# First edge gather of a graph network: sums kept with nodes on the lanes instead of features on the lanes

## Chip, cores and metric

The kernel is one program on one core of one Trainium2 chip, written instruction by instruction for each engine with explicit semaphores. The metric is device time in microseconds (us) of the whole program, the median of several executions.

## What is computed

The reference is a two-layer graph network on 6,250 nodes of 256 features: a message-passing layer over 100,000 edges, a mixture of 8 experts, a five-layer message-passing network over the same edges, and a second mixture whose gate is a graph attention over 65,536 edges. The part that the change touches is the first message passing:

```python
# x: (6250, 256); src, dst: (100000,); edge_weight: (100000,)
xn = _layernorm(x)
messages = xn[dst] * edge_weight[:, None]
agg = segment_sum(messages, src, num_segments=N)
h = xn + agg
out = relu(h @ W1 + b1) @ W2 + b2
x = x + out
```

Everything is in f32. What the change must deliver to the next stage is `h`, turned: `sh.agg` of shape [128, 2, 6272], with the feature within its block of 128 on the lanes (partitions), then the block of features, then the node.

## The kernel before

The program is a row of phases with a barrier of all engines between them; `first_sums` is the third, called p3 in the names of the profile. By then the edges are sorted by their target node into windows of 128 nodes (NT = 49 windows) and cut into NC1 = 832 chunks of 128 edges, each chunk within one window. `listA` holds for every edge the row to fetch, its place in its window and its weight.

`first_sums` walks the 832 chunks in 52 turns. A turn has S = 4 sets of U = 4 chunks. Each set has its own buffer `rows[s]` for fetched node rows, `hot[s]` for the matrices and `idx[s]` for the indices. The engines share the work like this:

- ACT (`Gather.act_set`) waits until TensorE has used up set s of the turn before (semaphore `used`, one count per chunk), then copies the four index columns to `idx[s]` (line 302).
- POOL (`Gather.pool_set`, line 308) waits for that copy, then issues four indirect DMAs, each of which fetches 128 rows of 1 KB of the table `xn0` to `rows[s][:, u, :]`.
- DVE (`Aggregate._matrices`, line 369) builds a 128x128 matrix for each chunk, which has the edge's weight at (edge, place in window), one set ahead; and (`_sums`, line 379) adds each finished product to the window of `sh.agg` that a register names. The registers are loaded four at a time (`windows_of`). Each add waits for the product and for the add before it.
- TensorE (`pe_set`, line 393) waits for the matrices (`hot_ready`), for the rows (`here`) and for each PSUM bank to be free (`added[u]`), and multiplies: for each of the two blocks of features the block of rows is the stationary operand and the matrix the moving one with 128 columns. The result has the features on the lanes and the nodes along them.
- The term `xn` itself comes in through `AddTurned`. In each of the first 49 turns SP loads one tile of 128 rows of `xn0` (two buffers), TensorE turns its two blocks (line 1802) after its own turn's products, and DVE adds them to `sh.agg` (line 1810) after its own turn's adds. TensorE's loop holds two turns for this, so that the two buffers alternate.

An f32 product or load of weights is recorded as two instructions, so a chunk shows four MATMUL and four LDWEIGHTS rows.

After the phase's barrier comes `first_ffn` (p4), whose `Ffn` reads `sh.agg`, while POOL issues scatters for a later stage (line 263).

## Time and profile before

| | |
|---|---|
| median of 3 runs | 14222.39 us (14183.71 to 14226.25) |
| the profiled execution: time, span | 14220.56 us, 14218.8 us |
| TensorE's granted clock, mean over the span | 0.766 |
| busy share of the span: PE, DVE, POOL, ACT | 53%, 46%, 52%, 9% |
| phase p3, from the memset's start to the last add's end | 1509.76 to 2800.40 us |
| in it: chunks, matmul rows, adds of line 379 | 832, 3328, 832 |

PE is TensorE's matmul row, PEld its loads of weights, DVE the vector engine, ACT the scalar engine, POOL the engine that issues the indirect DMAs, and SP the one that issues the plain ones. PEclk is the clock that TensorE was granted, as a share of 2.4 GHz. An idle time marked "issue" is one in which the engine waited for nothing that the profile shows; one marked "remote" has a releaser that the profile can't name.

### The profile page before, as it was taken

Reading aid. Unit: us, or ns where it says so; the run is one execution under the profiler, and the core shown is the slowest. Engines: PE = TensorE matmul, PEld = TensorE weight load, DVE = VectorE, ACT = ScalarE, POOL = GpSimd, SP = SyncE. Lnnn points to the kernel's source line nnn. Section 1 sums busy time; section 2 is a strip of 40 time slices with the busy share of each in tenths; the row PEclk is TensorE's granted clock in tenths of the full one; section 3 lists DMA queues with packets and bytes.
Section 4 is the critical chain, followed back from the end, with each engine's and each line's share of the span. In section 5 each row is a group of like instructions: output and inputs, shape, how many; then the busy total and the mean of one; then the engine's idle time right before and its main releaser. Section 6 shows DMA issues by size and latency. Waiting matters only on the chain. (4 is left out here: it accounts for less than half of the span.)

```text
span 14218.8 us, 158198 instructions
## 1 busy us (share of the span) xinstructions
PE 7586.1 (53%) x34918; PEld 5503.2 (39%) x34919; DVE 6529.1 (46%) x18936; ACT 1314.3 (9%) x3588; POOL 7369.4 (52%) x7692
## 2 busy tenths in 40 slices
PE   0002355552139677765655465555554655378877
PEld 0002344431026444444544344444443444233355
DVE  7336544411015356654444344434443444345566
ACT  0000000001001100001000100010001000123342
POOL 5772466635740255564666566656665666445400
PEclk9999866675569788877776777677776766578988
DMA  1000233211000133322333233323332333211203
GB/s 58 20 1 1 71 91 91 82 43 48 2 7 21 57 81 83 82 73 63 88 87 87 67 87 87 87 69 86 88 87 67 85 88 87 58 21 21 23 11 102
DMA packets 518785, 873.35 MB, mean 61 GB/s; under 512 B 180375, under 2 KB 355656, under 8 KB 517579
## 3 DMA queue, kind: packets, MB, share of 16 engines
q0 software_dynamic: 323968, 674.90, 18.6%
q1 hardware_dynamic: 194635, 196.60, 4.4%
q14 instruction: 138, 1.13, 0.0%
q8 instruction: 44, 0.72, 0.0%
HBM read 771.76 MB, written 105.62 MB: 62 GB/s over the span
## 5 line engine op out<-in xcount | busy, mean ns | idle before, releaser
L308 POOL DMA_INDIRECT p_layers_place<-nodesC,p_layers_idx x4160 | 3942.5, 948 | 2937.6 <-issue 1573.7
L393 PE MATMUL p_layers_bank<-p_layers_hots,p_layers_place 128*128 128x128 f32 x16640 | 3366.7, 362 | 2863.4 <-DVE agg L379 1513.9
L393 PEld LDWEIGHTS p_layers_bank<-p_layers_hots,p_layers_place 128*128 128x128 f32 x16640 | 2869.0, 257 | 3452.7 <-issue 1933.9
L379 DVE TENSOR_TENSOR agg<-agg,p_layers_bank 128x256 f32 x4160 | 1751.5, 421 | 2282.3 <-issue 858.9
L369 DVE TENSOR_SCALAR p_layers_hots<-iota,p_msg_edges 128x128 f32<-128x128 f32 x3328 | 997.6, 363 | 759.9 <-issue 599.8
L308 POOL DMA_INDIRECT p_gather_rows<-xn,p_gather_idx x832 | 788.3, 947 | 822.7 <-ACT p_gather_idx L302 578.6
L263 POOL DMA_INDIRECT listC<-h x782 | 777.1, 994 | 526.1 <-issue 253.0
L393 PE MATMUL p_agg_bank<-p_agg_hot,p_gather_rows 128*128 128x128 f32 x3328 | 685.9, 374 | 594.2 <-DVE agg L379 372.9
L263 POOL DMA_INDIRECT listA<-h x782 | 812.7, 1039 | 344.4 <-issue 341.0
L263 POOL DMA_INDIRECT listD<-recD,rowD x512 | 493.1, 963 | 785.3 <-issue 785.3
L393 PEld LDWEIGHTS p_agg_bank<-p_agg_hot,p_gather_rows 128*128 128x128 f32 x3328 | 602.8, 271 | 677.9 <-issue 373.6
L488 PE MATMUL p_ffn_y<-p_ffn_w,p_ffn_hid 128*128 128x256 f32 x1960 | 489.7, 409 | 649.9 <-issue 623.7
L302 ACT COPY p_layers_idx<-p_msg_edges 128x4 int32 x1040 | 203.0, 197 | 6378.9 <-PE p_layers_bank L393 2779.4
L1369 POOL DMA_INDIRECT gat_att_rows<-nodesD,gat_att_idx x560 | 529.2, 945 | 477.7 <-ACT gat_att_idx L1399 291.2
L488 PEld LDWEIGHTS p_ffn_y<-p_ffn_w,p_ffn_hid 128*128 128x128 f32 x1960 | 395.6, 205 | 753.1 <-issue 670.0
L530 DVE SCALAR_TENSOR_TENSOR p_ffn_acc<-p_ffn_y,p_mix_share,p_ffn_acc 128x256 f32<-128x256 f32 x392 | 189.4, 483 | 901.2 <-remote 591.4
L1642 DVE TENSOR_REDUCE gat_att_red<-gat_att_bank 128x4 f32<-128x512 f32 x560 | 373.8, 687 | 412.3 <-PE gat_att_bank L1481 200.6
L379 DVE TENSOR_TENSOR agg<-agg,p_agg_bank 128x256 f32 x832 | 350.3, 421 | 416.6 <-issue 165.8
L475 PE MATMUL p_ffn_pre<-agg,p_ffn_w 128*128 x1120 | 457.1, 562 | 137.7 <-ACT p_ffn_hid L509 68.3
L365 DVE SCALAR_TENSOR_TENSOR p_layers_hots<-iota,p_msg_edges,p_msg_dinv_row 128x128 f32<-128x128 f32 x832 | 273.5, 352 | 219.9 <-issue 132.0
L396 PE MATMUL p_layers_bank<-p_layers_hots,p_layers_attr 128*4 128x128 f32 x1664 | 364.7, 307 | 0.0
L475 PEld LDWEIGHTS p_ffn_pre<-agg,p_ffn_w 128*128 128x128 f32 x1120 | 222.7, 199 | 346.8 <-issue 271.5
(387 smaller groups left out, 8125.2 us busy)
## 6 DMA issues: line engine op xcount, KB each, us to landing
p_layers_place<-nodesC,p_layers_idx POOLq DMA_INDIRECT x4160
nodesC<-p_layers_place SPq DMA_DIRECT2D x24, 896.0 KB, 4.7
part_y<-rows SPq DMA_DIRECT2D x21, 896.0 KB
agg<-part_y SPq DMA_DIRECT2D x18, 896.0 KB, 10.3
p_gather_rows<-xn,p_gather_idx POOLq DMA_INDIRECT x832
x<-p_ffn_acc SPq DMA_DIRECT2D x14, 896.0 KB, 4.1
listA<-h POOLq DMA_INDIRECT x782
listC<-h POOLq DMA_INDIRECT x782
```

What stands on the lines that cost most here:

```text
L263: nc.gpsimd.indirect_dma_start(out=self.table, out_offset=bass.IndirectOffsetOnAxis(ap=self.row[0:n, t:t + 1], axis=0), in_=self.rec[0:n, ...
L302: nc.scalar.copy(self.idx[s], nodes).then_inc(self.ready[s], 1)
L308: nc.gpsimd.indirect_dma_start(out=self.rows[s][:, u, :], out_offset=None, in_=self.table, in_offset=bass.IndirectOffsetOnAxis(ap=self.idx ...
L365: ins = nc.vector.scalar_tensor_tensor(self.hot[s][:, u, :], self.sh.iota, place, self.by[:, ds(windows[u] * P, P)], ALU.is_equal, ALU.mul ...
L369: ins = nc.vector.tensor_scalar(self.hot[s][:, u, :], self.sh.iota, place, weight, ALU.is_equal, ALU.mult)
L379: nc.vector.tensor_tensor(to, to, prod, ALU.add).then_inc(self.added[u], 1)
L393: ins = nc.tensor.matmul(self.bank[u][:, f * P:(f + 1) * P], self.g.rows[s][:, u, f * P:(f + 1) * P], self.hot[s][:, u, :], start=True, st ...
L396: ins = nc.tensor.matmul(self.bank[u][0:4, D:D + P], self.attr[s][:, u, :], self.hot[s][:, u, :], start=True, stop=True)
L475: ins = nc.tensor.matmul(self.pre[j][:, m, 0:HW], self.w1[:, e, f, b * P:(b + 1) * P], self.tok[:, f, ds(g * GW + m * HW, HW)], start=(f = ...
L488: ins = nc.tensor.matmul(self.y[j][:, 0:D], self.hid[e % self.nh][:, b, s * P:(s + 1) * P], self.w2[:, e * HB + b, :], start=(b == 0), sto ...
L1369: nc.gpsimd.indirect_dma_start(out=self.rows[s][:, u, :], out_offset=None, in_=self.table, in_offset=bass.IndirectOffsetOnAxis(ap=self.idx ...
L1642: nc.vector.tensor_reduce(red[:, u, :], self.bank[u % 2].rearrange("p (a n) -> p a n", a=HEADS), AX.X, ALU.max).then_inc(self.reduced, 1)
```

## The change

`AddTurned` goes, and `RowSums`, a subclass of `Aggregate`, takes its place and that of the plain `Aggregate` in this phase. The five-layer network still uses the plain one.

- The product of a chunk has the matrix as the stationary operand and the fetched rows as the moving one: one product with 256 columns, whose result has the nodes on the lanes.
- The sums are kept in a new tile `a.agg` of [128, 49 * 256], nodes on the lanes. Each add reads and writes 256 elements in a row there.
- The tile of `xn0` for turn t is loaded by SP into one buffer, once the tile before has been added, and DVE adds it as it is.
- After the last chunk `pe_turn` turns each of the 49 windows (two transposes each, two PSUM banks in turn) and ACT copies each turned pair to `sh.agg` (`act_keep`).
- The edge list and the matrices `hot` are laid in the memory of `sh.agg`, which is free until the turning.
- TensorE's loop holds one turn instead of two.

```diff
-class AddTurned:
+class RowSums(Aggregate):
+    TURNED = 2
+
+    def __init__(self, sp, sh, g, edges, cw, own, take):
+        super().__init__(sp, sh, g, edges, cw, sp.sb("sums", [P, NP * FB]), place=False)
+        self.hot = [take(P, U, P) for _ in range(S)]
+        self.own = own
+        self.x = sp.sb("x", [P, D])
+        self.turn = [sp.ps(f"turn{j}", [P, FB, P]) for j in range(self.TURNED)]
...
     def sp(self, nc, sp):
+        with sp.Fori(0, NT) as t:
+            sp.wait_ge(self.own_added, START + t)
             hold(sp)
+            sp.dma_start(self.x, self.own[ds(t * P, P), :]).then_inc(self.own_here, 16)
+
+    def pe_set(self, nc, pe, it, s):
+        pe.wait_ge(self.hot_ready, START + it * S + (s + 1))
+        pe.wait_ge(self.g.here[s], it * (16 * U) + 16 * U)
+        for u in range(U):
+            pe.wait_ge(self.added[u], START + it * S + s)
+            nc.tensor.matmul(self.bank[u][:, 0:D], self.hot[s][:, u, :], self.g.rows[s][:, u, :], start=True,
+                             stop=True).then_inc(self.g.used, 1)
+
+    def _sums(self, nc, dve, it, i, s, edge_terms):
+        for u, w in enumerate(windows_of(nc, mybir.EngineType.DVE, self.cw, i * SU + s * U, U)):
+            dve.wait_ge(self.g.used, START + it * SU + (s * U + u + 1 + AHEAD))
+            dve.wait_ge(self.added[(u - 1) % U], START + it * S + s + (u > 0))
+            to = self.agg[:, ds(w * D, D)]
+            nc.vector.tensor_tensor(to, to, self.bank[u][:, 0:D], ALU.add).then_inc(self.added[u], 1)
+
+    def add_own(self, nc, dve, t):
+        dve.wait_ge(self.added[U - 1], START + (t + 1) * S)
+        dve.wait_ge(self.own_here, t * 16 + 16)
         hold(dve)
+        to = self.agg[:, ds(t * D, D)]
+        nc.vector.tensor_tensor(to, to, self.x, ALU.add).then_inc(self.own_added, 1)
+        dve.wait_ge(self.own_added, START + t + 1)
+
+    def pe_turn(self, nc, pe):
+        for u in range(U):
+            pe.wait_ge(self.added[u], START + NC1 // U)
+        pe.wait_ge(self.own_added, START + NT)
+        for t in range(NT):
+            j = t % self.TURNED
+            if t >= self.TURNED:
+                pe.wait_ge(self.kept, START + t - self.TURNED + 1)
+            for f in range(FB):
+                ins = nc.tensor.transpose(self.turn[j][:, f, :], self.agg[:, t * D + f * P:t * D + (f + 1) * P],
+                                          self.sh.ident)
+            ins.then_inc(self.turned, 1)
+
+    def act_keep(self, nc, act):
+        for t in range(NT):
+            act.wait_ge(self.turned, START + t + 1)
+            nc.scalar.copy(self.sh.agg[:, :, t * P:(t + 1) * P], self.turn[t % self.TURNED]).then_inc(self.kept, 1)
...
-            edges = sp_.sb("edges", [P, NC1, RA])
+            take = cut(sh.agg)
+            edges = take(P, NC1, RA)
-            a = Aggregate(space("agg"), sh, g, edges, cwA, sh.agg)
-            add = AddTurned(space("add"), sh, xn0)
+            a = RowSums(space("agg"), sh, g, edges, cwA, xn0, take)
...
-                    nc.vector.memset(sh.agg, 0.0).then_inc(zeroed, 1)
+                    nc.vector.memset(a.agg, 0.0).then_inc(zeroed, 1)
...
-                    with pe.Fori(0, NT // 2) as i:
-                        for j in range(2):
-                            turn(i * 2 + j)
-                            add.pe(nc, pe, i, j)
-                    turn(NT - 1)
-                    add.pe(nc, pe, NT // 2, 0)
-                    with pe.Fori(NT, g.turns) as i:
-                        turn(i)
+                    with pe.Fori(0, g.turns) as i:
+                        for s in range(S):
+                            a.pe_set(nc, pe, i, s)
+                    a.pe_turn(nc, pe)
```

## Rows read from the trace of the kernel before

**Rows 1.** Busy time by stage: stretch, length, engines' busy us (count), clock, DMA, GB/s.
```profile
1514.60:2788.20 1273.60, 690.36 (x3386) 607.23 (x3386) 617.95 (x1692) 39.70 (x204) 788.23 (x832) 0.70 0.31 90
```
**Rows 2.** Groups by line, 1520 to 2800: busy us, mean ns, idle before, releasers.
```profile
L308 POOL DMA_INDIRECT p_gather_rows<-xn,p_gather_idx x828 | 784.4, 947 | 484.4 <-issue 243.1 <-ACT p_gather_idx L302 241.3
...
L379 DVE TENSOR_TENSOR agg<-agg,p_agg_bank 128x256 f32 x832 | 350.3, 421 | 416.6 <-issue 165.8 <-PE p_agg_bank L393 105.9 <-remote 88.3
...
L1810 DVE TENSOR_TENSOR agg<-agg,p_add_turn 128x256 f32 x49 | 20.6, 421 | 31.1 <-issue 19.3 <-DVE agg L379 6.2 <-remote 5.6
```
**Rows 3.** Waits, 1520 to 2801: us in total, times, longest.
```profile
POOL p_gather_rows L308 <- ACT p_gather_idx L302: 241.3, 103, 4.7
```
**Rows 4.** Timeline, 2014 to 2024: start, us, engine, line, then idle before.
```profile
2014.58 0.38 PE L1802 MATMUL p_add_turn<-ident,p_add_x 128*128 128x128 f32 x2
2015.55 0.35 DVE L369 TENSOR_SCALAR p_agg_hot<-iota,p_sums_edges 128x128 f32<-128x128 f32 x1 [1.58 <-issue]
...
2022.04 0.42 DVE L379 TENSOR_TENSOR agg<-agg,p_agg_bank 128x256 f32 x1 [2.58 <-issue]
...
2022.77 0.20 ACT L302 COPY p_gather_idx<-p_sums_edges 128x4 int32 x1 [9.83 <-remote]
...
2022.91 0.33 SPq L1788 DMA_DIRECT2D p_add_x<-xn  x1
...
2023.73 0.94 POOL L308 DMA_INDIRECT p_gather_rows<-xn,p_gather_idx  x1 [3.27 <-ACT p_gather_idx L302]
```
**Rows 5.** Timeline of DVE, two sets of matrices in a quick stretch.
```profile
2056.67 1.21 DVE L369 TENSOR_SCALAR p_agg_hot<-iota,p_sums_edges 128x128 f32<-128x128 f32 x4
...
2060.54 1.11 DVE L369 TENSOR_SCALAR p_agg_hot<-iota,p_sums_edges 128x128 f32<-128x128 f32 x4
```
**Rows 6.** Line 369, DVE's sequencer instructions, 1980 to 2030: min/median/max ns.
```profile
L369 DVEq ALU_OP  x14: 2/40/700, 1986.2 to 2029.9; - x14
```
**Rows 7.** Busy time by stage at the end of a slow stretch; columns as in rows 1.
```profile
2022.00:2024.00 2.00, 1.49 (x7) 1.49 (x8) 1.26 (x3) 0.20 (x1) 0.27 (x1) 0.50 0.02 5
```
**Rows 8.** Timeline of TensorE, p5 and later, while POOL issues scatters throughout.
```profile
3464.95 3.62 PE L488 MATMUL p_ffn_y<-p_ffn_w,p_ffn_hid 128*128 128x256 f32 x16
3494.98 2.07 PE L488 MATMUL p_ffn_y<-p_ffn_w,p_ffn_hid 128*128 128x256 f32 x4 [26.41 <-issue]
3506.18 2.07 PE L488 MATMUL p_ffn_y<-p_ffn_w,p_ffn_hid 128*128 128x256 f32 x4 [9.13 <-issue]
```
**Rows 9.** Timeline of TensorE's weight loads in the gather.
```profile
2004.66 3.49 PEld L393 LDWEIGHTS p_agg_bank<-p_agg_hot,p_gather_rows 128*128 128x128 f32 x16 [10.58 <-DVE p_agg_hot L369]
2008.41 2.30 PEld L393 LDWEIGHTS p_agg_bank<-p_agg_hot,p_gather_rows 128*128 128x128 f32 x16 [0.27 <-issue]
```
**Rows 10.** Busy time by stage: clock for rows 8, 9 and 11; columns as in rows 1.
```profile
2008.40:2010.80 2.40, 2.35 (x16) 2.08 (x16) 1.84 (x6) 0.20 (x1) 1.79 (x3) 1.00 0.35 109
...
3460.00:3470.00 10.00, 8.57 (x30) 5.32 (x28) 0.48 (x1) 1.16 (x2) 7.56 (x9) 1.00 0.28 80
...
3490.00:3500.00 10.00, 2.07 (x4) 1.17 (x4) 0.88 (x2) 0.00 (x0) 7.56 (x9) 0.50 0.03 2
...
4797.90:4802.30 4.40, 4.04 (x14) 2.12 (x14) 4.25 (x13) 1.86 (x5) 3.48 (x4) 0.50 0.14 8
```
**Rows 11.** Timeline of a later norm, which turns tiles in the same way.
```profile
4797.92 4.40 PE L807 MATMUL msg_norm_turn<-ident,msg_norm_xn 128*128 128x128 f32 x14 [32.44 <-DVE msg_norm_xn L764]
4798.73 0.81 ACT L831 COPY h<-msg_norm_turn 128x256 f32 x2 [1.73 <-issue]
...
4799.97 0.82 ACT L831 COPY h<-msg_norm_turn 128x256 f32 x2 [0.42 <-issue]
```
**Rows 12.** Timeline of the norm before the first mixture, ACT's first copy of two tiles.
```profile
3195.83 0.37 ACT L830 COPY mix_norm_slot<-mix_norm_turn 128x256 f32<-128x256 f32 x1 [0.53 <-PE mix_norm_turn L807]
...
3197.00 0.37 ACT L830 COPY mix_norm_slot<-mix_norm_turn 128x256 f32<-128x256 f32 x1 [0.53 <-PE mix_norm_turn L807]
```
**Rows 13.** Timeline of DVE at the phase's end.
```profile
2799.98 0.42 DVE L379 TENSOR_TENSOR agg<-agg,p_agg_bank 128x256 f32 x1 [0.21 <-DVE agg L379]
```

More of the change, by code:

```diff
@@ L1770, in dve @@
         self.gate.dve(nc, dve, link)
-class AddTurned:
-    def __init__(self, sp, sh, table):
-        self.sh, self.table = sh, table
-        self.x = [sp.sb(f"x{j}", [P, D]) for j in range(2)]
-        self.turn = sp.ps("turn", [P, 512])[:, 0:D]
-        self.here = [sp.sem(f"here{j}", dma=True) for j in range(2)]
-        self.turned, self.added = sp.sem("turned"), sp.sem("added")
+class RowSums(Aggregate):
[6 more added lines that the diff above has]
+        self.turn = [sp.ps(f"turn{j}", [P, FB, P]) for j in range(self.TURNED)]
+        self.own_here = sp.sem("own_here", dma=True)
+        self.own_added, self.turned, self.kept = sp.sem("own_added"), sp.sem("turned"), sp.sem("kept")
@@ L1784, in sp @@
     def sp(self, nc, sp):
-        def load(t, j, n):
-            sp.wait_ge(self.turned, START + t - 1) if n is None else sp.wait_ge(self.turned, START)
+        with sp.Fori(0, NT) as t:
+            sp.wait_ge(self.own_added, START + t)
             hold(sp)
-            sp.dma_start(self.x[j], self.table[ds(t * P, P), :]).then_inc(self.here[j], 16)
-        load(0, 0, 0)
-        load(1, 1, 0)
-        with sp.Fori(1, NT // 2) as i:
-            for j in range(2):
-                load(i * 2 + j, j, None)
@@ L1794, in sp @@
-        load(NT - 1, (NT - 1) % 2, None)
-    def pe(self, nc, pe, i, j):
-        t = i * 2 + j
-        pe.wait_ge(self.here[j], i * 16 + 16)
-        pe.wait_ge(self.added, START + t)
-        hold(pe)
-        for f in range(FB):
-            ins = nc.tensor.transpose(self.turn[:, f * P:(f + 1) * P], self.x[j][:, f * P:(f + 1) * P],
-                                      self.sh.ident)
-        ins.then_inc(self.turned, 1)
-    def dve(self, nc, dve, t):
-        dve.wait_ge(self.turned, START + t + 1)
-        hold(dve)
-        to = self.sh.agg[:, :, ds(t * P, P)]
-        nc.vector.tensor_tensor(to, to, self.turn.rearrange("p (f n) -> p f n", f=FB), ALU.add).then_inc(self.added, 1)
+            sp.dma_start(self.x, self.own[ds(t * P, P), :]).then_inc(self.own_here, 16)
@@ L2044, in _ @@
                     sp.dma_start(edges.rearrange("p c w -> p (c w)"), lanes(listA)).then_inc(here, 16)
-                    add.sp(nc, sp)
+                    a.sp(nc, sp)
                 @block.scalar
```

10 lines of the change are left out of this document (2 added, 8 removed).

## Prediction, made before the changed kernel was run

> **What bounds the kernel now.** The change touches one phase, so I first cut it out with the view by stages. The reader is to see that from the first gather to the last, 1273.6 us, POOL issues 832 gathers and is busy for 788.2 us, the largest share of any engine, with TensorE at 690 us and DVE at 618 us, and that none of them is full [rows 1]. The groups of the phase say what lies between: a gather takes 947 ns, and POOL's idle time is 243.1 us of "issue", which is the gap between two gathers, and 241.3 us of waiting for the copied indices [rows 2]. That is 788 + 243 + 241 = 1272 us: POOL is in a row with itself except for 103 pauses of 2.3 us [rows 3]. Without the pauses a chunk costs (788 + 243) / 832 = 1.24 us, with them 1.53 us. So POOL's own pace, 832 x 1.24 = 1031 us, is a floor that this change does not move, and the pauses are all that it can win in the loop.
>
> Next the timeline, for what makes a pause. In quick stretches DVE starts the matrices of a set every 3.87 us [rows 5], which is 15.5 us for a turn of four sets, where POOL needs 16 x 1.24 = 19.8 us. DVE would be early. But there are slow stretches. In one, DVE builds a matrix at 2015.55 and makes its next add only at 2022.04, "issue" being the reason [rows 4]; its sequencer's register instructions take up to 700 ns there where the median is 40 [rows 6]. ACT and SP have nothing of the sort to issue and are late too: TensorE turned its tile at 2014.58, and SP, which waits for just that, starts its load at 2022.91; ACT copies its indices at 2022.77; POOL, which had nothing left to issue, resumes at 2023.73 after 3.27 us [rows 4]. The DMA share tells when this ends: it is 0.31 over the phase [rows 1], and 0.02 at 2022 to 2024 [rows 7]. DVE, ACT and SP all move again when POOL has run dry and its transfers have drained. The same is seen far from here, in a phase where POOL scatters without end: TensorE does four products, idles 9.13 us, does four more [rows 8]. I read this as one thing: while POOL issues indirect DMAs in an unbroken row, what the other engines signal each other comes late, and DVE's sequencer crawls. I cannot name the mechanism. What matters is that the loop's pace is a cycle of POOL running, the others falling behind, POOL pausing, the others catching up, and that the time in which DVE gets on is spent on DVE's own work and not on waits for TensorE: of DVE's 416.6 us idle before its adds, 105.9 us over 210 times fall to TensorE's products [rows 2], half a microsecond each.
>
> **The change, part by part.**
>
> *One product of 256 columns for two of 128.* The row of a 128-column product in this loop: 16 loads of weights (four chunks) span 2.30 us at a granted clock of 1.00, so 0.144 us an instruction and 0.58 us a chunk [rows 9, 10]. At the lower level the 16 span 3.49 us, 0.218 us each, 0.87 us a chunk [rows 9]. For 256 columns, the product nearest in kind is that of the dense layer: 16 instructions in 3.62 us at a clock of 1.00, 0.226 us each, so 0.45 us for the two that a chunk will need; 4 in 2.07 us at 0.50, at most 0.52 us each, and 0.44 if the columns alone set it, 0.87 us a chunk [rows 8, 10]. The array streams the same number of columns; only what is saved at the high level counts, 0.13 us a chunk. The clock's mean of 0.70 [rows 1] lies 40% of the way from 0.5 to 1, so if all of it counted the phase would win 832 x 0.4 x 0.13 = 43 us. I take 0: a set costs TensorE at most 4 x 0.87 = 3.5 us against DVE's 3.87 us, so DVE's work covers it; were DVE that much faster, the 43 us would be there.
> The Trainium skill says, in "Perfetto Trace Analysis", Optimizing Tensor Performance, that larger matmuls are more efficient than smaller ones; the rows agree at the high clock and not at the low one, and taken as the rule of this loop it would give those 43 us.
>
> *DVE's adds and matrices.* 832 adds at 421 ns and 832 matrices stay, with as many elements, the same waits and the same register loads. An add now goes to 256 elements in a row instead of two runs of 128; both are f32 from PSUM and I take no change. The add of the own tile (49 at 421 ns, 31.1 us idle before them [rows 2]) stays as one add with as many waits, now for a DMA instead of for TensorE. At most it gives back its idle time, 31 us, and at least nothing, since the crawl is in DVE's sequencer and hits this add as any other. I take 5 us.
>
> *The transposes in the loop* leave TensorE: 98 of them, a pair in 0.38 us [rows 4], which DVE's work covered. Taken into the previous term's 5 us.
>
> *SP's load* has one buffer instead of two. It is issued after the add of turn t-1 and needed 24 us later. SP can be late by 8 us (2014.58 to 2022.91 [rows 4]), then the load lands. It fits with more than 10 us to spare, so 0; behind this wait DVE's whole next turn is queued, so if it did not fit it would cost in each of 49 turns.
>
> *Memset* has the same size, and the matrices moved into `sh.agg` cost nothing.
>
> *The turning at the end* is new and nothing hides it: it starts after the last add (now at 2799.98 [rows 13]) and the barrier waits for it. 49 tiles, each two transposes and a copy of 128x256 from PSUM by ACT. A later norm does exactly this with two banks: TensorE's seven pairs span 4.40 us and ACT's copies come two at a time, 4798.73 and 4799.97, so 1.24 us for two tiles, 0.62 us a tile [rows 11]. That is at a granted clock of 0.50 [rows 10]. 49 x 0.62 = 30.4 us. The lower bound: at the high clock a pair takes 0.38 us [rows 4] and the copy about 0.37 us [rows 12], so ACT alone would set some 0.45 us, 22 us in all. The upper bound: no overlap between pair and copy, as in the norm with a head, 1.17 us a tile (3195.83 to 3197.00 [rows 12]), 57 us. I take 30, the row nearest in kind, plus 1 us for the first pair to fill.
> The Trainium skill says in "TensorE: Matmul & The Clock Gate", Part 4, that transposes do not bring the clock up. The norm's 0.50 agrees with it, and by it the end costs 30 us; if the clock were up, 22 to 25.
>
> *Sum.* 0 - 5 + 30 + 1 = +26 us. The profiled execution took 14220.56 us (1.8 us less than the median), so 14247 by it, and 14222.4 + 26 = 14248 by the median.
>
> **The rivals.**
>
> *A, the pauses shrink* (faster). TensorE's loop becomes half as long, its products of a chunk end in one instruction pair instead of two, and the pair of transposes no longer stands between turns. If that broke the cycle of running and pausing, up to 241 us would go [rows 3], and with +31 at the end the time would be about 14222 - 241 + 31 = 14012. For it: everything in the loop is a chain of signals. Against it: the slow stretches are in DVE, ACT and SP, whose instructions do not change, and they appear just as much where the products are already 256 wide [rows 8]. A half measure, TensorE's 43 us and the 31 us before the own add, gives 31 - 74 = -43 us, 14179.
>
> *B, the end is dearer or the loop a little slower* (slower). At the upper bound of 57 us the time is 14222 + 57 = 14279; the point from which it decides is 0.88 us a tile, at which 49 tiles cost 43 us. It would come about if TensorE's next pair waited for the copy before it in each bank with the signals' delay on top. For it: each bank is handed to and fro. Against it: the norm with the same hand-over shows 0.62, and POOL is idle by then, so signals are prompt.
>
> *C, another rhythm.* A cycle of pauses can settle into another pattern: 103 pauses in 52 turns are two a turn. Half a pause more or less a turn is 26 x 2.34 = 61 us either way, so 14187 or 14309. Nothing in the profile says which.
>
> **How the numbers follow.** What a measurement here can tell from no change is about 0.3%, 43 us. Forecast, within 14220 to 14275: 0.46. A: 0.10 in full or in large part, 0.06 by half. B: 0.16. C: 0.22, half to each side. The range takes in B, C on both sides and A's half, 14150 to 14312, and leaves out A in full and the extremes, less than 2 in 10. The forecast's own range is 14235 to 14262. Faster by over 0.3%: A in full 0.10, half of A's half 0.03, and two thirds of C's faster side with what B's end takes off, 0.07, so 0.20. Slower: C's slower side 0.11, B past 0.88 us a tile 0.10, and 0.05 of the forecast's upper tail, so 0.26. Within: 0.54.
>
> **What would show it right or wrong.** In the profile of the changed kernel: line 302's pauses for POOL near 241 us and two a turn; POOL's last gather about 1273 us after its first; DVE's sets 3.87 us apart in quick stretches; register instructions of 700 ns as before; TensorE's two instructions a chunk 0.21 us apart at the high clock; and at the end 49 pairs and copies 0.6 us apart, with a clock near 0.5, in 30 us. The prediction is wrong if the pauses go or double, if DVE is seen waiting for `own_here` at the ends of turns, or if the last 49 tiles take over 0.9 us each.

## The result: 1.5% slower

| | before | changed |
|---|---|---|
| median, us | 14205.36 (4 runs, 14183.71 to 14226.25) | 14418.30 (4 runs, 14351.07 to 14460.91) |
| ratio | | 1.0146, 95% interval 1.0102 to 1.0190 |
| profiled execution, us | 14220.56 | 14351.07 |

The forecast was 14248 us within 14150 to 14312, so the time lies outside the range, on the slow side. The profiled execution of the changed kernel is the quickest of its four, and every number of the changed kernel below that comes from a trace is of that one.

The phase by itself, by stage and by groups. The first is busy time by stage, as in [rows 1]; the second has the groups, as in [rows 2]; the third the waits, as in [rows 3].

```profile
1521.80:2987.50 1465.70, 620.32 (x1642) 351.72 (x1642) 614.26 (x1691) 39.72 (x204) 787.59 (x832) 0.70 0.27 79
```

```profile
L308 POOL DMA_INDIRECT p_gather_rows<-xn,p_gather_idx x832 | 787.6, 947 | 1017.0 <-ACT p_gather_idx L302 775.6 <-issue 241.4
L1802 PE MATMUL p_agg_bank<-p_gather_rows,agg 128*128 128x256 f32 x1642 | 620.8, 515 | 854.2 <-DVE p_agg_sums L1810 650.3 <-issue 108.0 <-DVE agg L369 94.9
...
L1810 DVE TENSOR_TENSOR p_agg_sums<-p_agg_sums,p_agg_bank 128x256 f32 x817 | 344.4, 421 | 339.9 <-issue 189.2 <-PE p_agg_bank L1802 99.7 <-DVE p_agg_sums L1810 40.3
L369 DVE TENSOR_SCALAR agg<-iota,agg 128x128 f32<-128x128 f32 x824 | 244.8, 351 | 439.6 <-issue 423.2 <-PE p_agg_bank L1802 12.2 <-DVE p_agg_sums L1817 0.8
...
L1817 DVE TENSOR_TENSOR p_agg_sums<-p_agg_sums,p_agg_x 128x256 f32 x49 | 21.0, 428 | 71.1 <-issue 46.3 <-PE p_agg_bank L1802 21.9 <-DVE p_agg_sums L1810 2.9
```

```profile
POOL p_gather_rows L308 <- ACT p_gather_idx L302: 436.7, 58, 9.7
ACT p_gather_idx L302 <- PE p_agg_bank L1802: 1242.7, 176, 17.8
ACT p_gather_idx L302 <- issue: 167.6, 27, 8.4
...
ACT p_gather_idx L302 <- remote: 6.7, 1, 6.7
```

From the first gather to the last the phase grew from 1273.6 us [rows 1] to 1465.7, by 192 us. With the turning behind it, the last of the phase's work ends at 3022.3 us instead of 2800.4, 222 us later (7 of them lie ahead of the first gather), which is about the 213 us between the medians. (The two profiled executions differ by 131 us only, since all that follows took 11327 us in the changed kernel's and 11418 in the other's; no edit touches that part.) A gather still takes 947 ns and the gaps between gathers are 241.4 us, so POOL's own pace has not moved. What grew is its waiting for indices: 436.7 us against 241.3 [rows 3], a difference of 195 us. (The 775.6 of the group includes the 338.9 us ahead of the very first gather.) And it changed its form: 103 pauses of 2.3 us became 58 of 7.5, the longest 9.7. DVE has as much work as before (an add 421 ns, a matrix 0.35 us), but idles 439.6 us ahead of its matrices (212.3 before), 423.2 of it for nothing that the profile shows. Its register instructions there, as in [rows 6], count and min/median/max ns:

```profile
L369 DVEq ALU_OP  x357: 1/40/708, 1528.5 to 2977.3; - x179
```

One turn of the changed kernel, in the timeline. The columns are start, us, engine, line, then the idle time before in brackets.

```profile
2047.14 0.94 POOL L308 DMA_INDIRECT p_gather_rows<-xn,p_gather_idx  x1 [9.56 <-ACT p_gather_idx L302]
...
2048.64 0.19 ACT L302 COPY p_gather_idx<-agg 128x4 int32 x1 [2.26 <-PE p_agg_bank L1802]
...
2052.47 0.19 ACT L302 COPY p_gather_idx<-agg 128x4 int32 x1 [3.64 <-PE p_agg_bank L1802]
...
2057.01 0.19 ACT L302 COPY p_gather_idx<-agg 128x4 int32 x1 [4.35 <-PE p_agg_bank L1802]
...
2058.45 0.43 DVE L1817 TENSOR_TENSOR p_agg_sums<-p_agg_sums,p_agg_x 128x256 f32 x1 [2.32 <-issue]
...
2064.75 0.35 DVE L369 TENSOR_SCALAR agg<-iota,agg 128x128 f32<-128x128 f32 x1 [5.88 <-issue]
2065.88 0.95 POOL L308 DMA_INDIRECT p_gather_rows<-xn,p_gather_idx  x1 [0.30 <-issue]
2066.89 0.35 DVE L369 TENSOR_SCALAR agg<-iota,agg 128x128 f32<-128x128 f32 x1 [1.79 <-issue]
...
2070.52 0.42 DVE L1810 TENSOR_TENSOR p_agg_sums<-p_agg_sums,p_agg_bank 128x256 f32 x1 [0.44 <-issue]
...
2074.70 0.19 ACT L302 COPY p_gather_idx<-agg 128x4 int32 x1 [17.50 <-PE p_agg_bank L1802]
...
2075.67 0.94 POOL L308 DMA_INDIRECT p_gather_rows<-xn,p_gather_idx  x1 [8.85 <-ACT p_gather_idx L302]
```

POOL resumes at 2047.14 and issues sixteen gathers without a pause, the last at 2065.88. For the first eight us or so everybody is quick: ACT copies indices at 2048.64, 2052.47 and 2057.01, so POOL has permission for three more sets. From 2055 on DVE crawls, that is, it does its work at a fraction of its pace: the own add at 2058.45, the next matrix 5.88 us after it, the four matrices of the set spread over 5 us. It is quick again at 2070.5, soon after POOL's transfers have drained (the DMA share is 0.41 between 2067 and 2068 us, 0.03 in the next microsecond and 0.00 then). But no permission is in store now: the next set of gathers needs DVE and TensorE to finish real work, which they do until 2074.7, and POOL has stood for 8.85 us.

In the kernel before the same slow stretch ends otherwise. There the copy of indices itself is late (9.83 us, "remote" [rows 4]): it is made at 2022.77, though TensorE's last products before it had ended at 2014.74 and given their permission. POOL runs dry sooner, and when the transfers have drained the copy is made at once and POOL is back after 3.27 us [rows 4]. "Remote" was the reason for 59 of the copies between 1550 and 2750 in the trace of before, and for one in the whole phase of the changed kernel. So the kernel before paid for its slow stretches in short pauses, and the changed kernel pays in long ones.

The turning at the end, in the timeline and by stage:

```profile
2999.25 0.42 DVE L1810 TENSOR_TENSOR p_agg_sums<-p_agg_sums,p_agg_bank 128x256 f32 x1 [0.21 <-DVE p_agg_sums L1810]
2999.92 0.63 PE L1829 MATMUL p_agg_turn<-ident,p_agg_sums 128*128 128x128 f32 x4 [2.41 <-DVE p_agg_sums L1810]
3000.37 0.65 ACT L1836 COPY agg<-p_agg_turn 128x256 f32<-128x256 f32 x2 [22.12 <-PE p_agg_turn L1829]
...
3001.27 0.65 ACT L1836 COPY agg<-p_agg_turn 128x256 f32<-128x256 f32 x2 [0.25 <-PE p_agg_turn L1829]
...
3021.97 0.37 ACT L1836 COPY agg<-p_agg_turn 128x256 f32<-128x256 f32 x1 [0.25 <-PE p_agg_turn L1829]
```

```profile
3000.00:3022.00 22.00, 17.48 (x98) 9.71 (x98) 0.00 (x0) 15.66 (x49) 0.00 (x0) 1.00 0.00 1
```

Two tiles every 0.90 us, so 22 us in all, where the sum had 31. The granted clock was 1.00 throughout.

### The profile page after: what moved, and what is told of

Read it like the earlier page. It is cut to its first block and busy times, and to the rows that moved or that the text cites. A ratio compares the mean times of both kernels' runs of the same rounds, so it can differ in the third digit from the quotient of the medians.

```text
span 14349.4 us, 154916 instructions
## 1 busy us (share of the span) xinstructions
PE 7536.6 (53%) x33254; PEld 5254.9 (37%) x33255; DVE 6528.0 (45%) x18936; ACT 1330.3 (9%) x3637; POOL 7373.6 (51%) x7692
## 5 line engine op out<-in xcount | busy, mean ns | idle before, releaser
L308 POOL DMA_INDIRECT p_gather_rows<-xn,p_gather_idx x832 | 787.6, 947 | 1017.0 <-ACT p_gather_idx L302 775.6
L1802 PE MATMUL p_agg_bank<-p_gather_rows,agg 128*128 128x256 f32 x1664 | 629.8, 516 | 854.7 <-DVE p_agg_sums L1810 650.3
L1802 PEld LDWEIGHTS p_agg_bank<-p_gather_rows,agg 128*128 128x128 f32 x1664 | 357.5, 246 | 1126.8 <-DVE agg L369 573.7
L1810 DVE TENSOR_TENSOR p_agg_sums<-p_agg_sums,p_agg_bank 128x256 f32 x832 | 350.7, 421 | 344.7 <-issue 191.6
L369 DVE TENSOR_SCALAR agg<-iota,agg 128x128 f32<-128x128 f32 x832 | 247.0, 351 | 439.6 <-issue 423.2
```

What stands on the lines that cost most here:

```text
L308: nc.gpsimd.indirect_dma_start(out=self.rows[s][:, u, :], out_offset=None, in_=self.table, in_offset=bass.IndirectOffsetOnAxis(ap=self.idx ...
L369: ins = nc.vector.tensor_scalar(self.hot[s][:, u, :], self.sh.iota, place, weight, ALU.is_equal, ALU.mult)
L1802: nc.tensor.matmul(self.bank[u][:, 0:D], self.hot[s][:, u, :], self.g.rows[s][:, u, :], start=True, stop=True).then_inc(self.g.used, 1)
L1810: nc.vector.tensor_tensor(to, to, self.bank[u][:, 0:D], ALU.add).then_inc(self.added[u], 1)
```

## The experiments

The kernel before, run on the same chip with each, took 14302.86 us for e1 to e4, 14220.20 for e5 to e8, 14163.61 for e9 to e12, 14299.25 (median of 19) for e13 to e16, and 10772.47 (median of 7) for e17 and e18, of which more below. These are four chips, and the changed kernel itself was traced only for the result, not again beside any of the experiments. Two executions of the whole kernel can differ by some 90 us in the phases that no edit touches, so for most runs I read the stretch from the first gather to the last, in the profile. Where a run has one execution (all but e14, e15, e16 and e18), a stretch is one reading: two products gave 1285.1 and 1293.2 us in e3 and e15, the same kernel on two chips.

### Which part of the change does it (e1 to e4)

```diff
 # e1: kernel before, this in place of its two products in the first gather
+nc.tensor.matmul(self.bank[u][:, 0:D], self.hot[s][:, u, :], self.g.rows[s][:, u, :], start=True,
+                 stop=True).then_inc(self.g.used, 1)
 # e2: changed kernel (e3: the same with hot as first operand and rows as second)
+for f in range(FB):
+    ins = nc.tensor.matmul(self.bank[u][:, f * P:(f + 1) * P], self.g.rows[s][:, u, f * P:(f + 1) * P],
+                           self.hot[s][:, u, :], start=True, stop=True)
+ins.then_inc(self.g.used, 1)
 # e4: changed kernel, POOL two sets ahead instead of three, in the wait and in what the counter starts with
+dve.wait_ge(self.g.used, START + it * SU + (s * U + u + 1 + AHEAD - U))
+nc.tensor.sem_inc(g.used, AHEAD - U)
```

e1 and e2 change what is computed, though not its amount: the product comes out with nodes and features exchanged against the sums that it is added to. e3 and e4 compute everything.

> The kernel before with only the product changed: the matrix is the stationary operand and the fetched rows the moving one with 256 columns, as in the changed kernel; the own tile, the adds and the layout stay as they were, so the sums that it adds are laid out wrongly. Theory (signals): the loop's rhythm is set by which operand is stationary; with the matrix stationary the counts of used chunks come at once, POOL gets all four sets in a row, issues 16 gathers unbroken and then pauses once a turn for some 9 us. Then the gathers' stretch here takes 1440 to 1490 us like that of the changed kernel (1466), not 1274 as before. Rival (own tile): the added time comes from the own tile's load in one buffer and its add at the end of the turn; then this stretch stays at 1250 to 1300 us. Rival (end): all of it is the turning; excluded if the stretch itself moves.

> The changed kernel with only the product put back: two products of 128 columns with the fetched rows stationary; what it adds is then laid out wrongly. Theory (signals): POOL's pauses are short again, two a turn, and the stretch of gathers falls from 1466 to 1250 to 1300 us, the turning at the end stays at 22 us. Rival (own tile): the stretch stays at 1440 to 1490 us.

> The changed kernel with each chunk's product cut into two of 128 columns, the matrix still stationary and loaded twice. This tells the width of the product from the choice of the stationary operand. If the operand decides (the fetched rows' semaphore no longer stands before a load of weights), the stretch stays at 1440 to 1490 us; if the width or the number of TensorE's instructions decides, it falls towards 1274 us.

> The changed kernel with POOL allowed two sets (8 chunks) ahead of TensorE instead of three, in this phase alone. Theory (unbroken row): DVE's sequencer crawls from some 7 us after POOL begins an unbroken row of gathers until it stops; with shorter rows the crawls are short or gone, and the stretch falls below 1466 us, to 1200 to 1350, though POOL pauses more often. Rival (a fixed place in DVE's loop costs the crawl, whatever POOL does): fewer sets ahead can only add waiting, the stretch is 1466 us or more and each turn still has a crawl of some 14 us at its end.

Measured, busy time by stage from the first gather to the last, e1, e3:

```profile
1544.50:2948.00 1403.50, 657.41 (x1738) 369.03 (x1738) 609.13 (x1690) 39.73 (x204) 788.97 (x832) 0.69 0.28 82
```

```profile
1521.60:2806.70 1285.10, 711.70 (x3295) 626.04 (x3296) 619.74 (x1699) 39.70 (x204) 788.81 (x832) 0.68 0.30 90
```

The kernel before, with nothing but one product instead of two, goes to 1403.5 us (whole kernel 14428.24): 130 of the 192 us, and less than the 1440 to 1490 that I expected. The changed kernel with two products comes back to 1285.1 us (e3, 14292.78) or 1293.0 (e2, 14279.83), whichever operand is stationary. That operand was my first suspect; it has no part in it. Nor have the layout of the sums, the own tile or the memory under `sh.agg`, all of which e2 and e3 keep. By themselves these are worth 12 to 20 us (1285.1 to 1293.2 against 1273.6). It is the one product for two, which costs 130 us in the kernel before and 173 to 181 in the changed one; what makes the difference between the two, no run shows. In the view of waits ACT's copies tell the two kinds apart: between 1600 and 2780 the trace of e3 has 58 copies "remote", 480 us, and POOL's pauses are short; e1 has 11, and long pauses.

e4 brought nothing: 1486.4 us of gathers, 14477.70 in all, one pause of 9.5 to 10 us a turn as in the changed kernel, only four gathers earlier in the turn. By what was expected this speaks for the rival, a fixed place in DVE's loop; but half of POOL's rows were still of sixteen gathers, so the row had not been shortened, and the question went to e8.

### Width, number or time of the products (e5, e6, e7, e13)

```diff
 # e5: the product of 256 made twice, the second counted
 # e6: four products of 64 columns, the last counted
 # e7: ahead of the product of 256, which is counted
+nc.tensor.matmul(self.bank[u][:, D:D + 8], self.hot[s][:, u, :], self.g.rows[s][:, u, 0:8], start=True, stop=True)
 # e13: behind the product of 256, which is counted
+nc.tensor.sem_inc(self.spare, 1)
+nc.tensor.sem_inc(self.spare, 1)
```

> The changed kernel with its product of 256 columns made twice per chunk into the same bank, the second one counted: no more is computed, TensorE has twice the work and twice the instructions. Theory 1 (the number of TensorE's instructions per chunk decides whether POOL has many short pauses or one long one a turn): the gathers take 1280 to 1310 us as with two products of 128. Theory 2 (the width of a product decides, wide ones are bad by themselves): 1400 to 1470 us as with one. Theory 3 (the time at which the chunk is counted): the counts come about 1 us later per chunk than with one product, and the stretch is 1466 us or more.

> The changed kernel with four products of 64 columns per chunk instead of one of 256. Theory 1 (number of instructions): 1280 to 1310 us of gathers, or shorter yet. Theory 2 (width): the same or shorter. Theory 3 (the count comes late): about as long as one product of 256 or longer, 1466 us. A stretch outside of all that would mean that neither orders the cases and that the rhythm is a matter of chance.

> The changed kernel with a product of 8 columns into a spare part of the bank ahead of each product of 256, which is still the one that is counted: the output does not use it. Theory 1 (number of instructions, whatever their width): 1280 to 1310 us of gathers. Theory 2 (width of the counted product): 1400 to 1470 us. Theory 3 (TensorE's busy time and so the time of the count): nearly as with one product, 1440 to 1470 us.

> The changed kernel with two increments of a spare semaphore on TensorE's queue after each product, which compute nothing. Theory 7 (what counts is how many instructions TensorE has to fetch per chunk, so that its counts come late while POOL issues in an unbroken row, ACT's copy is late, and POOL's row ends early): the gathers take 1280 to 1320 us, as with two products. Theory 8 (it is the products themselves, by their weight loads and the time that they hold TensorE): 1400 to 1470 us, as with one.

Measured, by stage, e7, then e6:

```profile
1521.90:2805.00 1283.10, 1017.22 (x3285) 834.52 (x3286) 615.26 (x1697) 39.71 (x204) 789.85 (x832) 0.55 0.30 90
```

```profile
1521.80:2932.90 1411.10, 1399.23 (x6557) 1398.86 (x6557) 608.76 (x1693) 39.69 (x204) 787.74 (x832) 1.00 0.27 82
```

| | products a chunk | gathers, us | pauses of POOL for indices, us (times) | whole kernel, us (kernel before on that chip) |
|---|---|---|---|---|
| changed | 256 | 1465.7 | 436.7 (58) | 14351.07 (14220.56) |
| e5 | 256, 256 | 1311.6 | 286.8 (116) | 14228.65 (14220.20) |
| e7 | 8, 256 | 1283.1 | 210.1 (88) | 14214.84 (14220.20) |
| e3 | 128, 128 | 1285.1 | 248.4 (97) | 14292.78 (14302.86) |
| e6 | 64, 64, 64, 64 | 1411.1 | 413.9 (193) | 14348.79 (14220.20) |
| e13 | 256, two increments | 1406.3 | 333.4 (76) | 14425.44 (14299.25) |

(The pauses of e3 to e13 are the wait's total less that ahead of the first gather.)

A product of 8 columns whose result nobody reads takes 183 us off. So width does no harm by itself (theory 2 falls), and a count that comes later does none either: e5 and e7 both count later than the changed kernel and are faster (theory 3 falls). e6 is a case of its own: TensorE is busy 1399 of 1411 us, the pace is TensorE's, 27.3 us for each turn, POOL rests 2.1 us after every set, and between 1600 and 2700 us none of line 369's ALU_OPs, the register instructions of [rows 6], takes more than 40 ns. That "more products are better yet" is thereby refuted, and it points the same way as e8 below: regular rests of POOL, no crawl. e13's increments lengthen TensorE's code without a product and win 59 of the 183 us, with no late copy between 1600 and 2780. The 1406.3 us are what was expected if the products themselves matter (1400 to 1470); instructions to fetch are not what counts, or not mainly.

### Breaking POOL's row (e8 to e12)

```diff
 # e8, e9, e10: 1120, 280, 16 columns, changed kernel; e12: 280, kernel before; e11: 1120, after every second set
 g.pool_set(nc, pool, i, s)
+nc.gpsimd.memset(spare, 0.0).then_inc(gapped, 1)
+pool.wait_ge(gapped, START + i * S + (s + 1))
```

> The changed kernel with a memset of 1120 columns on POOL (about 1 us) after each set of four gathers and a wait for it, so that gathers never follow one another for more than 5 us. 52 turns of 4 gaps are 208 x 1.1 = 229 us of added POOL time. Theory 4 (the slow stretches come from an unbroken row of indirect transfers, longer than about 7 us): the slow stretches of DVE and the long pauses of 9 us go, pauses on ready fall from 437 us to under 60 and the stretch is 1031 + 229 + 60, some 1320 us or less instead of 1466. Theory 5 (a place of its own in the loop's turn decides): the pauses stay at 9 us a turn and the stretch becomes about 1466 + 229 = 1695 us less what the gaps take over, no less than 1500 us.

> The kernel with the gap on POOL after each set of four gathers, the memset a quarter as wide (280 columns, by the 1.04 us of 1120 some 0.3 us; with the wait behind it a gap of about 0.8 us more than the usual step). Theory 4 (what matters is that a row of indirect transfers ends before the slow stretch begins, some 7 us after its start, and any rest does): no pauses for the idx tile, a turn of 19.8 + 4 x 0.8 = 23.1 to 23.6 us, the gathers take 1200 to 1230 us. Theory 6 (the rest must be long enough for what has piled up to drain, 2 us or so): slow stretches come back, pauses of several us in most turns, 1280 us or more.

> The same with a memset of 16 columns (under 0.1 us), so that the gap is nearly the wait alone, about 0.6 us more than the usual step. Theory 4: a turn of 22.2 to 22.8 us, 1155 to 1185 us of gathers. Theory 6: slow stretches and pauses as in the changed kernel, 1400 us or more.

> The changed kernel with the gap of 1120 columns only after every second set, so that eight gathers (10 us) stand in an unbroken row, past the 7 us after which DVE slowed in the traces. Theory 4: slow stretches of about 3 us in every row, with late signals: pauses come back, the turn lies above 19.8 + 2 x 1.55 = 22.9 us, at 24 to 27 us (1250 to 1400 us). Theory 5 (a place of its own in DVE's loop decides, and the gap helps only because it slows POOL): pauses of up to 9 us a turn, 1450 us or more. If the turn is 22.9 us without pauses, a row of ten us does no harm.

> The kernel before with the gap of 280 columns after each set. Theory 4: the slow stretches go here as well, since they do not come from the products; the gathers take 1200 to 1230 us instead of 1274, about as long as in the changed kernel with the same gap. Theory 1 in its strong form (the number of TensorE's instructions sets the pace by itself): a difference of 100 us or more to the changed kernel with the same gap.

Measured. By stage, e9 and then e12; behind each, the sequencer instructions of line 369 (count, then min/median/max ns, over 1600 to 2700):

```profile
1522.10:2767.10 1245.00, 704.10 (x1656) 475.81 (x1656) 612.78 (x1710) 39.71 (x204) 862.83 (x1040) 0.62 0.31 93
```

```profile
L369 DVEq ALU_OP  x321: 40/40/40, 1603.3 to 2696.2; - x161
```

```profile
1515.00:2759.80 1244.80, 717.19 (x3410) 663.44 (x3410) 613.12 (x1710) 39.68 (x204) 862.71 (x1040) 0.63 0.31 93
```

```profile
L369 DVEq ALU_OP  x321: 40/40/40, 1602.2 to 2696.2; - x161
```

And the pauses of e9, by waits (the second row is the wait ahead of the first gather, and only that):

```profile
POOL p_gather_rows L308 <- issue: 380.5, 829, 2.1
POOL p_gather_rows L308 <- ACT p_gather_idx L302: 339.1, 1, 339.1
POOL p_gather_rows L308 <- POOL p_sums_spare L2088: 1.6, 2, 0.8
```

A rest in e9, in the timeline of POOL:

```profile
2100.39 0.95 POOL L308 DMA_INDIRECT p_gather_rows<-xn,p_gather_idx  x1 [0.30 <-issue]
2101.34 0.34 POOL L2088 MEMSET p_sums_spare<- 128x280 f32 x1
2102.48 0.95 POOL L308 DMA_INDIRECT p_gather_rows<-xn,p_gather_idx  x1 [0.80 <-issue]
```

This rest, which computes nothing and makes a step 2.09 us long instead of 1.25, 0.84 more, makes the whole loop 221 us faster: every pause is gone, and no ALU_OP of line 369 takes over 40 ns where the changed kernel has 708 and before 700 [rows 6]. With it the number of products is worth nothing: 1245.0 us with one and 1244.8 with two. So the product acts only by way of the pauses. In the whole kernel e9 took 14175.48 us, e10 14178.98, e11 14193.86 and e12 14119.27, against 14163.61 for the kernel before; e8 took 14297.98 against 14220.20.

How long a rest is needed: with 1120 columns (e8) 1388.9 us, no pause, the rests themselves too dear (26.5 us a turn). With 16 columns (e10) a step after four gathers takes 1.88 us, 0.63 more than the usual one, and the loop 1224.8 us, 20 less than in e9; but sequencer instructions of 711 ns and 17 pauses (36.6 us) are back. They are no rarity: 385 ALU_OPs and FUSED_REGOPS of DVE's sequencer take more than 0.3 us in e10's gathers, 423 in the changed kernel's, 38 in e11's, none in those of e8, e9 and e12. So a rest can take nearly all the pauses away while the slow instructions stay. The 1155 to 1185 us that theory 4 gave it were not reached, so a rest needs some length to keep the slow instructions away, as theory 6 held, though not the 2 us that it named; for the loop's time the shorter rest was the better one. With 1120 columns after every second set (e11) 1228.3 us, no pause for indices, though single register instructions of 709 ns are there and DVE idles 131 us of "issue" ahead of its adds between 1600 and 2700: a row of 10 us touches the slow stretch and ends before it does harm. The times themselves missed what theory 4 gave them: e8 was to take 1320 us or less, e9 and e12 1200 to 1230, e11 1250 to 1400. That the pauses would go was right. Theory 5, a place of its own in DVE's loop, falls: DVE goes through the same loop in e8, e9 and e12.

### Sizes, with an interval (e14, e15, e16)

> The kernel before with the gap of 280 columns after each set of gathers of the first gather, timed. Theory 4: 1274 us become 1245, as in one look, so the median is 20 to 40 us under the kernel before (ratio 0.997 to 0.9985). No rival expects a gain; if the 1245 us are eaten up later, the ratio is 0.999 to 1.001.

> The changed kernel with two products of 128 columns, everything else as changed, timed. If the single wide product is the whole cause, the stretch of the gathers is 1284 us against 1274, the turning at the end adds 22 us, and the ratio to the kernel before is 1.000 to 1.004; if the layout of the sums costs something by itself outside of the first gather, it is over 1.006.

> The kernel before with the same gap in every gather of this form, those of the five layers too (1040 sets more). In the trace of before POOL pauses there for 1367 us in 594 pauses; a gap costs about 0.75 us more than the usual step, 1040 x 0.75 = 780 us. Theory 4 holds in general: all pauses go and the kernel becomes up to 590 + 29 = 620 us shorter (ratio 0.957 to 0.975). If TensorE or DVE, which have more to do per chunk in the layers, set the pace there, little is gained: 0.98 to 1.01; if the gaps come on top, 1.03 and more.

| | median, us | ratio to before, 95% interval | gathers, us |
|---|---|---|---|
| e14, before, gap in the first gather | 14259.24 (10 runs) | 0.9970 (0.9955 to 0.9984) | 1245.6 |
| e15, changed, two products of 128 | 14331.28 (10 runs) | 1.0016 (0.9996 to 1.0036) | 1293.2 |
| e16, before, gap in all gathers | 13921.65 (4 runs) | 0.9734 (0.9718 to 0.9751) | 1244.9 |

The ratios all fell within what was expected. e15 is the forecast's own number: without the single product the rest of the change costs 0.16%, 23 us with an interval of -6 to +51, where the sum had +26. The agreement is in part luck: in e15's trace the gathers take 20 us more than in the kernel before, where the sum had 5 less, and the turning 22 us instead of 31. e16 is faster than both kernels: the same edit in the pool's loop of all gathers, e16's diff being

```diff
     def pool_set(self, nc, pool, it, s):
...
+        nc.gpsimd.memset(self.spare, 0.0).then_inc(self.gapped, 1)
+        pool.wait_ge(self.gapped, START + it * S + (s + 1))
```

The pauses in the layers, by waits, first before, then e16:

```profile
POOL p_layers_place L308 <- ACT p_layers_idx L302: 1363.9, 598, 6.9
```

```profile
POOL p_layers_place L309 <- ACT p_layers_idx L303: 191.8, 103, 2.1
```

103 pauses are left there, and the kernel is 378 us faster where up to 620 were expected. On this chip the same rest also did less in the first gather than in e12. In e16 POOL never pauses there for indices, apart from the wait ahead of the first one, and yet ACT's copies are marked "remote" as often as in the kernel before (the second row, over 1600 to 2700):

```profile
POOL p_gather_rows L309 <- ACT p_gather_idx L303: 361.6, 1, 361.6
ACT p_gather_idx L303 <- remote: 396.8, 62, 9.9
```

Register instructions of DVE take up to 710 ns in e14 and 717 in e16. Counted as for e10, 65 of some 4130 take more than 0.3 us in each of the two, against 326 in the kernel before and none in e12. So here the rest made the slow stretches fewer and kept POOL from pausing, but it did not remove them. Whether that is the chip or chance, two traces on each of two chips don't say.

### Another chip (e17, e18)

```diff
 # e17: changed kernel, the product 384 columns wide, its neighbour chunk's 128 columns are not added
+lo = max(0, u * D - P)
+nc.tensor.matmul(self.bank[u][:, 0:D + P], self.hot[s][:, u, :],
+                 self.g.rows[s].rearrange("p u d -> p (u d)")[:, lo:lo + D + P], start=True,
+                 stop=True).then_inc(self.g.used, 1)
 # e18: e16 with the gap after every second set
+if s % 2:
```

> The changed kernel with its one product per chunk 384 columns wide instead of 256; the 128 columns more are those of a neighbouring chunk and are not added. It has two instructions of TensorE per chunk as before, but holds TensorE half as long again: at the low clock, by e5 (0.85 us for 256 columns), 1.28 us per chunk, the same as the 8 + 256 columns of e7. Theory 9 (TensorE's pace: after a pause it hands out the chunks about as slowly as POOL issues, 1.24 us, so that POOL does not get 16 gathers in one row): 1280 to 1320 us of gathers. Theory 8 (the number of products or weight loads): 1400 to 1470 us as with one product of 256.

> The kernel before with the gap of 280 columns in every gather of this form, but only after every second set: rows of eight gathers (10 us). Against e16 this takes 624 gaps of about 0.75 us away, 470 us. If rows of 10 us do no more harm in the layers than the 0.5 us a turn that e11 showed in the first gather: 470 - 312 x 0.5 = 310 us less than e16, a ratio to the kernel before of about 0.952 (0.945 to 0.965). If the slow stretches come back in the layers, where DVE and TensorE have less room, or if these set the pace there: 0.97 to 0.99.

These two ran on a chip on which the kernel before took 10772.47 us (10768.75 to 10781.25 in 7 runs), not 14160 to 14300. e17 took 10802.02, e18 11425.44, a ratio of 1.0607 (1.0589 to 1.0625). By stage, the sequencer instructions of line 369, and POOL's waits for indices over the whole kernel, e17:

```profile
1155.40:2197.80 1042.40, 741.97 (x1656) 363.21 (x1656) 606.68 (x1710) 39.70 (x204) 789.14 (x832) 0.84 0.37 111
```

```profile
L369 DVEq ALU_OP  x357: 40/40/47, 1162.1 to 2178.6; - x179
```

```profile
POOL p_gather_rows L308 <- ACT p_gather_idx L302: 45.7, 112, 11.9
POOL p_layers_place L308 <- ACT p_layers_idx L302: 65.7, 147, 2.5
```

POOL issues in an unbroken row for the whole phase (20.0 us for each turn of sixteen), and nothing crawls: 47 ns at most for an ALU_OP of line 369. The gathers take 1042.4 us, which is the floor of 1031 us of the prediction and little more. A gather takes 948 ns, as everywhere. So in the two traces from this chip there are no slow stretches, and a gap only costs: 624 gaps of e18 are 653 us more, 1.05 us each. It also means that e17 could not tell what it was made for. It shows something else: without slow stretches the changed kernel, with a product of 384 columns, took 10802.02 us in its one execution against 10772.47, 30 us more, close to the +26 of the sum.

## Why the prediction was wrong

**POOL's pace as the floor, the pauses as all that can move**: right. 947 ns and 241 us of gaps stayed, and the other chip's 1042 us show the floor itself.

**The slow stretches, and what brings them** ("while POOL issues indirect DMAs in an unbroken row"): right as far as POOL's row goes, by intervention now (e8, e9, e12) and not by reading alone. In e10, e14 and e16 slow instructions remain although POOL rests every four gathers, so an unbroken row is not all of it: the length of the rest counts, and perhaps the chip.

**One product for two, taken at 0 with a bound of -43 us**: this is the step that failed. The stretch of the gathers grew by 192 us in the profile; e3 and e15, with two products again, give 181 and 173 of it back, and the single product put into the kernel before costs 130 (e1). The term was priced as work, TensorE's time under DVE's cover, and as work it is worth nothing, as said (1245.0 against 1244.8 us in e9 and e12). What was left out is that in this loop TensorE's instructions also set how long POOL's row gets, and with it the pause: 1465.7 us and rows of sixteen gathers with one product, some 1290 us and rows of eight or twelve with two. No upper side was given to the term at all. Of the signs that the prediction named, the pauses were to be near 241 us and two a turn; they are 437 us and one a turn. The Trainium skill says in "Perfetto Trace Analysis", Optimizing Tensor Performance, that larger matmuls are more efficient. The prediction weighed that with the same 43 us; e9 and e12 show nothing of it in the loop's time, and without the rests the larger product lost.

**Rival C, another rhythm**: the idea is the right one, but its size was off, and by its own arithmetic the sign too. It was priced at half a pause of 2.34 us a turn, 61 us, so that 45 pauses fewer would have made the loop 105 us faster. The number of pauses fell, from 103 to 58; it is their length that rose, from 2.3 to 7.5 us. Taking the mean pause of before as a constant was the error: the pause depends on what is in store when the transfers have drained, 3.3 us if a permission waits to be copied [rows 4], 9 if DVE and TensorE must first earn it (8.85 in the turn above). The timeline of before had part of the means for that: a set takes DVE 3.87 us in a quick stretch [rows 5], and two such sets are 7.7. With one pause of 9 us a turn instead of two short ones, 52 x (9 - 4.6) = 229 us would have stood as the upper bound. That is an estimate made after the result, and no run was made to test it.

**DVE's adds and the own add, -5 us**: not earned. The adds take 421 ns as before; the idle time ahead of the 49 own adds is 71.1 us, against 31.1 [rows 2], 46.3 of it "issue", as in the turn shown, where the add stands in the crawl.

**SP's one buffer, 0**: right; in the view of waits no wait of DVE in the phase is put down to that load.

**The turning, 31 us**: 22 us, the lower bound of the term. The forecast took the pace of the norm at a granted clock of 0.50 [rows 10, 11]; here the clock stood at 1.00 when the first transpose began, and stayed there for the 22 us. In e3 it had fallen to 0.50 just before the first transpose and stayed there, and the turning took 28 us. The level is thus worth 6 us; the prediction had named it (22 to 25 us if the clock were up) and taken the other one. Rival B, a dearer end, did not come about: a tile cost 0.45 us. The Trainium skill says in "TensorE: Matmul & The Clock Gate", Part 4, that transposes don't bring the clock up. The 0.50 over e3's 28 us agrees with it. In the changed kernel they did not let it fall either.

**Rival A** (the pauses shrink): they grew. That all of them can be removed, e12 and e14 show, but the rests cost most of what the pauses give: 29 us of the 241 are left (1273.6 to 1244.8).

**What stays open.** Why one product leads to rows of sixteen and two products to rows of eight or twelve. The traces show the link, ACT's copies "remote" or not, and that e7's product of 8 columns is enough to bring it. Whether it works by the number of products, or by the time they hold TensorE (in e7 1.28 us a chunk at a clock of 0.50, about POOL's 1.24), was to be told by e17 and was not. Nor do the runs say by what path POOL's row slows the others' registers and signals. The number of instruction packets that the DMA queues moved is as small in the changed kernel as in e17 (156 both, over the whole kernel), so the loops are not fetched again and again. It is open why one chip of those used has none of it, and why DVE and ACT are still slow at times in e14 and e16. Every execution here was recorded for its span and clock, and no run shows whether the slow stretches depend on that.

## What to carry to other kernels

A loop whose pace is a cycle of running ahead and standing still must not be priced by its mean pause: ask what is in store when the stalled engine is released, and give every edit, even one that takes work off a covered engine, a bound for a cycle that locks in at its worst phase. Where POOL issues indirect DMAs in a row and other engines show register instructions of 0.7 us or copies with late signals, try a short rest of POOL every four gathers, try more than one length, and measure it on the chips that the kernel is to run on: here a rest in all gathers was worth 2.7% on one chip (e16), and half as many cost 6% on another (e18).

## What the hardware did that I had not expected

- While POOL issues indirect DMAs in an unbroken row of more than about 7 us, DVE's register instructions take 0.7 us instead of 0.04, and signals reach ACT and SP some 8 us late (2014.74 to 2022.77 and 2014.58 to 2022.91 in the kernel before), until the transfers have drained. In the changed kernel's trace POOL stands still for over 0.7 us 56 times; 55 of the 57 rows between hold a register instruction of over 0.3 us, and in eight of ten of these rows the first comes 6.2 to 8.4 us after the row's start. With 0.84 us of rest after every four gathers (5 us) there was none in e9 and e12 on one chip; in e14 and e16 on another 65 remained, with no pause of POOL. With a memset of 16 columns 385 remained (e10), with a rest after every eight gathers 38 (e11), and POOL hardly paused in either.
- Of the chips used, one shows none of this in its two traces, and the kernel before takes 10772 us there instead of 14160 to 14300. In the two gather loops of e17 the pauses for indices are 34 us (111 of 0.3 us each) and 66, where the changed kernel had 437 in the first and the kernel before 1364 in the other; whether all of the 3.4 ms is of this kind was not shown. The gather itself takes 948 ns there and 947 here.
- A useless product of 8 columns ahead of each product of 256 made the loop 183 us faster (e7).
